# Experts' rows weighted on ScalarE and added by the scatter into two DRAM tables

## The reference

```python
topk_w, topk_i = jax.lax.top_k(tmp_scores, K)               # T x 6
flat = topk_i.reshape(-1)
pos = jnp.sum(jnp.cumsum(oh, axis=0) * oh, axis=-1) - 1     # oh: one-hot of flat
slot = flat * C + jnp.minimum(pos, C - 1)                   # C = 96
buf = jnp.zeros((E * C, H), x.dtype).at[slot].set(x[tok]).reshape(E, C, H)
g = jnp.einsum('ech,emh->ecm', buf, Wg)
u = jnp.einsum('ech,emh->ecm', buf, Wu)
out = jnp.einsum('ecm,ehm->ech', jax.nn.silu(g) * u, Wd).reshape(E * C, H)
yk = out[slot].reshape(T, K, H)
y = jnp.sum(yk * topk_w[..., None], axis=1)
return y + shared          # shared: one dense expert that all tokens pass
```

## Time and profile before

| | before |
|---|---|
| median of 3 runs, us | 1561.48 (1559.58 to 1565.09) |
| span of the profiled execution, us | 1556.1 |
| PE busy, us | 1394.1 (90%) |
| DVE busy, us | 1047.9 (67%) |
| ACT busy, us | 814.5 (52%) |
| POOL busy, us | 374.1 (24%) |
| DMA moved | 215.08 MB, mean 138 GB/s |
| of it on POOL's queue (q0) | 36.90 MB, 8.0% of 16 engines' span |

### The profile page before, as it was taken

The page is one execution under the profiler, slowest core; times in us unless marked ns, Lnnn a source line. Parts: engine busy times, 40 slices in busy tenths (PEclk is TensorE's granted clock), DMA queues, the critical chain, the costliest instruction groups (busy, mean ns, idle before and its releaser), DMA issues. The chain is left out here.

```text
span 1556.1 us, 36410 instructions
## 1 busy us (share of the span) xinstructions
PE 1394.1 (90%) x12869; PEld 982.9 (63%) x12869; DVE 1047.9 (67%) x2191; ACT 814.5 (52%) x1682; POOL 374.1 (24%) x796
## 2 busy tenths in 40 slices
PE   3848999999679999999989999999998798799977
PEld 2414555554556777777777677777767745599963
DVE  4856777764778888888822888888882378422228
ACT  1316665655327877777711877787770116222330
POOL 0434665530021111111110101111101000577730
PEclk9969999999889999999999999999999799799985
DMA  3038999872025655565620665566651430599948
GB/s 101 1 68 170 248 246 248 214 160 52 1 79 113 143 138 138 133 142 133 138 59 1 129 141 134 135 142 138 138 128 31 133 95 1 162 290 288 289 135 295
DMA packets 463401, 215.08 MB, mean 138 GB/s; under 512 B 412082, under 2 KB 434448, under 8 KB 463072
## 3 DMA queue, kind: packets, MB, share of 16 engines
q1 hardware_dynamic: 448992, 175.09, 47.0%
q0 software_dynamic: 12000, 36.90, 8.0%
q10 hardware_dynamic: 2336, 2.16, 0.4%
HBM read 81.97 MB, written 31.52 MB: 73 GB/s over the span
## 5 line engine op out<-in xcount | busy, mean ns | idle before, releaser
L1073 PE MATMUL bank<-a_pt,v_part 128*128 128x128 f16 x3456 | 235.3, 220 | 13.9 <-DMA a_pt<-a_ph 8.9
L1136 ACT ACTIVATE a_ph<-a_p,a_rinv 128x1024 f16<-128x1024 f32 (+7 forms) x256 | 198.7, 777 | 79.3 <-POOL a_rinv L1015 75.7
L755 DVE TENSOR_REDUCE a_qh<-bank 128x1 f16<-128x1024 f32 (+7 forms) x256 | 182.3, 755 | 85.0 <-PE bank L645 83.3
L1073 PEld LDWEIGHTS bank<-a_pt,v_part 128*128 128x128 f16 x3456 | 208.9, 98 | 47.2 <-DVE z_part L1163 7.5
L1144 DVE TENSOR_REDUCE a_negm<-bank 128x1 f32<-128x1024 f32 (+7 forms) x256 | 191.7, 749 | 55.9 <-PE bank L1057 55.7
L1052 PE MATMUL bank<-a_k,a_q 128*128 128x512 f16 (+3 forms) x1152 | 228.7, 326 | 0.2
L743 ACT ACTIVATE a_p<-bank 128x1024 f32<-128x1024 f32 (+7 forms) x256 | 157.8, 649 | 128.7 <-PE bank L700 113.3
L1178 DVE SCALAR_TENSOR_TENSOR a_ph<-a_p,a_rinv,a_ph 128x1024 f16<-128x1024 f32 (+7 forms) x256 | 206.8, 808 | 1.7 <-ACT a_ph L1136 1.7
L1125 ACT ACTIVATE a_p<-bank,a_negm 128x1024 f32<-128x1024 f32 (+7 forms) x256 | 189.3, 739 | 21.6 <-DVE a_negm L1144 21.6
L1015 POOL TENSOR_TENSOR a_rinv<-a_rinv,p_scale 128x1 f32<-128x1 f32 x256 | 48.8, 191 | 610.6 <-DVE a_rinv L1157 610.4
L924 PE MATMUL bank<-x_part,wsplit 128*128 128x512 f16 x768 | 186.0, 379 | 4.1 <-PEq L199 1.8
(11 more groups left out here) (206 smaller groups left out, 2230.9 us busy)
## 6 DMA issues: line engine op xcount, KB each, us to landing
wgu<-in_wgu SPq DMA_DIRECT2D x64, 352.0 KB
choice_rows<-zero POOLq DMA_DIRECT2D x24, 512.0 KB, 4.9
c_rows<-choice_rows SPq DMA_DIRECT2D x16, 768.0 KB, 11.2
wsplit<-w_parts POOLq DMA_DIRECT2D x30, 384.0 KB, 3.8
wd<-in_wd SPq DMA_DIRECT2D x64, 176.0 KB
pw_in<-in_wqkv SPq DMA_DIRECT2D x16, 384.0 KB, 4.9
w_parts<-pw_part SPq DMA_DIRECT2D x16, 384.0 KB, 2.9
a_pt<-a_ph SPq DMA_TRANSPOSE x256, 3.0
```

Source lines behind the costliest of these rows:

```text
L755: dve.tensor_reduce(qh[s][:, i, MC:MC + 1], s1_place(t), AX.X, ALU.max, negate=True).then_inc(m_ready, 1)
L1073: ins = eng.matmul(Z_ps[:, cols], g.vs[par][v_][:, k, :], turned[slot][:, a * blocks[j] + k, :], start=(k == 0 and (v_, a) == PARTS[0]), s ...
L1136: eng.activation(parts[slot][:, 0:w_], probs[slot][:, 0:w_], ACT.Copy, scale=rinv[:, p_, jj:jj + 1]).then_inc(p_hi, 1)
```

## The change

`choice_rows` goes. In its place stand two DRAM tables `token_sums0` and `token_sums1`, with one row per token and 128 spare rows. The scatter of expert e adds its rows into table e % 2 (`compute_op=ALU.add`), and before it is issued GpSimd waits until the previous scatter into that table, that of expert e - 2, has landed. Empty slots and the last slot now go to the spare rows.

So that rows can be added, they must be weighted first. `token_rows` gets 64 more columns and is doubled: its first half holds each token's `masked_scores`, the second half, which the last slot gathers from, holds ones. ScalarE's evacuation takes the expert's column of the gathered row as its scale. The normalized rows are therefore written twice, in eight transfers, and two further SyncE transfers write the 64 columns in the router.

The gather for expert e + 16 no longer waits for TensorE's transposes. The zeros are 10 writes in place of 24 (eight of 512 KB and two of 128 KB). In the tail SyncE loads two tiles of one table at a time, 16 transfers of 256 KB; GpSimd adds the two tables' parts, VectorE adds the late tokens' share from TensorE (eight tiles of it ahead) and then GpSimd's sum. The diagonal matrices and the multiply-adds go.

```diff
-        g.zero = sb("zero", [P, K * T * D // P // ZD])
-        g.xrows = nc.dram_tensor("token_rows", (T, D), F32, kind="Internal").ap()
-        g.krows = nc.dram_tensor("choice_rows", (K * T, D), F32, kind="Internal").ap()
+        g.zero = sb("zero", [P, 4 * D])
+        g.xrows = nc.dram_tensor("token_rows", (2 * T, D + E), F32, kind="Internal").ap()
+        g.sums = [nc.dram_tensor(f"token_sums{a}", (T + P, D), F32, kind="Internal").ap() for a in range(2)]
...
                 if kind == "keep":
-                    xv = g.xrows.rearrange("(n p) d -> p n d", p=P)
+                    xv = g.xrows.rearrange("(a n p) d -> a p n d", p=P, a=2)[:, :, :, 0:D]
                     for q in range(4):
                         sp.wait_ge(s_xn, N0 + 4 * q + 4)
-                        sp.dma_start(xv[:, 4 * q:4 * q + 4, :], xn[:, 4 * q:4 * q + 4, :]).then_inc(s_kept, 16)
-                    sp.wait_ge(s_kept, 64)
+                        for a in range(2):
+                            sp.dma_start(xv[a, :, 4 * q:4 * q + 4, :], xn[:, 4 * q:4 * q + 4, :]).then_inc(s_kept, 16)
+                    sp.wait_ge(s_kept, 128)
...
-                zv = g.krows.rearrange("(z p n) d -> z p (n d)", p=P, z=ZD)
+                def clear(z):
+                    rows = g.sums[z % 2][z // 2 * 4 * P:min(z // 2 * 4 * P + 4 * P, T + P), :]
+                    n = rows.shape[0] // P
+                    pool.dma_start(rows.rearrange("(p n) d -> p (n d)", p=P),
+                                   g.zero[:, 0:n * D]).then_inc(g.s_zero, 16)
...
-                        pool.dma_start(zv[m - 4], g.zero[:, :]).then_inc(g.s_zero, 16)
+                        clear(m - 4)
...
+            sp.wait_ge(s_msc, 1)
+            wv = g.xrows.rearrange("(a n p) d -> a p n d", p=P, a=2)[:, :, :, D:D + E]
+            sp.dma_start(wv[0], msc[:, :, :]).then_inc(s_kept, 16)
+            sp.dma_start(wv[1], ones[:, :].unsqueeze(1).to_broadcast([P, NT, E])).then_inc(s_kept, 16)
...
+            dve.nop().then_inc(s_msc, 1)
...
             dve.wait_ge(s_used, K)
-            dve.tensor_copy(g.src[:, :], picked[:, 0, :])
-            chained(dve.tensor_copy(dtmp[:, 0, :], picked[:, 0, :]))
-            chained(dve.scalar_tensor_tensor(dtmp[:, 0, :], picked[:, 1, :], float(T), dtmp[:, 0, :],
-                                             ALU.mult, ALU.add))
-            chained(dve.tensor_scalar(dtmp[:, 1, :], picked[:, 1, :], 0.5, float(OOB), ALU.is_lt, ALU.mult))
-            chained(dve.scalar_tensor_tensor(dtmp[:, 0, :], dtmp[:, 1, :], last[0:C, 0:1], dtmp[:, 0, :],
-                                             ALU.add, ALU.add))
+            dve.tensor_scalar(g.src[:, :], picked[:, 0, :], last[0:C, 3:4], None, ALU.add)
+            dve.tensor_scalar(dtmp[:, 0, :], picked[:, 0, :], last[0:C, 0:1], last[0:C, 2:3], ALU.mult, ALU.add)
+            chained(dve.tensor_scalar(dtmp[:, 1, :], picked[:, 1, :], 0.5, last[0:C, 1:2], ALU.is_lt, ALU.mult))
+            chained(dve.tensor_tensor(dtmp[:, 0, :], dtmp[:, 0, :], dtmp[:, 1, :], ALU.add))
...
+            pool.wait_ge(s_kept, 32)
...
-    rows = [g.sb(f"x_rows{i}", [C, XG, D], F32, c) for i in range(XB // XG)]
+    rows = [g.sb(f"x_rows{i}", [C, XG, D + E], F32, c) for i in range(XB // XG)]
...
             for i in range(NR):
-                sp.wait_ge(s_scat[i], ROWS_IN * (E // XB))
                 sp.wait_ge(s_out[i], 16 * (E // XB) + 16)
             c_load(sp)
...
-                                        bounds_check=T - 1, oob_is_err=False).then_inc(s_row[e % XB // XG], 16)
+                                        bounds_check=2 * T - 1, oob_is_err=False).then_inc(s_row[e % XB // XG], 16)
             for e in range(XB):
                 gather(e)
             for e in range(E):
                 pool.wait_ge(s_o, e + 3)
-                pool.indirect_dma_start(out=g.krows, out_offset=bass.IndirectOffsetOnAxis(
+                if e >= 2:
+                    pool.wait_ge(s_sum[e % 2], 16 * (e // 2))
+                pool.indirect_dma_start(out=g.sums[e % 2], out_offset=bass.IndirectOffsetOnAxis(
                     ap=g.dst[:, e:e + 1], axis=0), in_=orow[e % XB // XG][:, e % XG, :], in_offset=None,
-                    bounds_check=K * T - 1, oob_is_err=False).then_inc(s_scat[e % XB // XG], 16)
+                    compute_op=ALU.add).then_inc(s_sum[e % 2], 16)
                 if e >= XG and e % XG == 2:
-                    done = e // XG - 1
-                    pool.wait_ge(s_scat[done % NR], ROWS_IN * (done // NR + 1))
+                    for a in range(2):
+                        pool.wait_ge(s_sum[a], 16 * (XG // 2) * (e // XG))
                     pool.nop().then_inc(s_free, 1)
                 if e + XB < E:
-                    pool.wait_ge(s_t, e // 2 + 1)
                     gather(e + XB)
-            for i in range(NR):
-                pool.wait_ge(s_scat[i], ROWS_IN * (E // XB))
+            for a in range(2):
+                pool.wait_ge(s_sum[a], 16 * E // 2)
+            c_pair(pool)
...
-                act.activation(orow[s // XG][:, s % XG, :], g.bank[2][0:C, s % 2, 0:D], ACT.Copy).then_inc(s_o, 1)
+                act.activation(orow[s // XG][:, s % XG, :], g.bank[2][0:C, s % 2, 0:D], ACT.Copy,
+                               scale=rows[s // XG][:, s % XG, ds(e + D, 1)]).then_inc(s_o, 1)
...
 def combine(g, c, out):
-    NB = 8
-    rows = [g.sb(f"c_rows{i}", [P, K, D], F32, c) for i in range(NB)]
+    NQ = NT // 2
+    part = [[g.sb(f"c_sums{a}_{q}", [P, 2, D], F32, c) for q in range(NQ)] for a in range(2)]
     last = g.sb("c_last", [E, D], F32, c)
-    s_g = [g.sem(f"c_load{i}") for i in range(NB)]
-    s_acc, s_st, s_l, s_mm, s_dg, s_xs = [g.sem(f"c_{n}") for n in ("acc", "store", "last", "mm", "diag", "sum")]
+    s_in = [g.sem(f"c_load{q}") for q in range(NQ)]
+    s_st, s_l, s_mm, s_ov, s_pair, s_x = [g.sem(f"c_{n}") for n in ("store", "last", "mm", "overflow", "pair", "sum")]
+    g.s_sum = [g.sem(f"x_sum{a}") for a in range(2)]
     ov = out.rearrange("b (n p) d -> p (b n) d", p=P)
-    kv = g.krows.rearrange("(k n p) d -> p n k d", n=NT, p=P)
+    sv = [g.sums[a][0:T, :].rearrange("(n p) d -> p n d", p=P) for a in range(2)]
+    def overflow_bank(t):
+        return g.bank[t % 8 // 2][:, t % 2, 0:D]
     def load(sp):
         sp.dma_start(last[:, :], g.lrows).then_inc(s_l, 16)
-        for t in range(NT):
-            if t >= NB:
-                sp.wait_ge(s_xs, t - NB + 1)
-            sp.dma_start(rows[t % NB][:, :, :], kv[:, t, :, :]).then_inc(s_g[t % NB], 16)
+        def fetch(a, q):
+            sp.dma_start(part[a][q][:, :, :], sv[a][:, 2 * q:2 * q + 2, :]).then_inc(s_in[q], 16)
+        sp.wait_ge(g.s_sum[0], 16 * E // 2)
+        fetch(0, 0)
+        sp.wait_ge(g.s_sum[1], 16 * E // 2)
+        fetch(1, 0)
+        for q in range(1, NQ):
+            for a in range(2):
+                fetch(a, q)
     def matmul(pe):
         pe.wait_ge(s_l, 16)
         for t in range(NT):
-            if t >= 4:
-                pe.wait_ge(s_xs, t - 3)
-            ps = g.bank[t % 4][:, 0, 0:D]
-            pe.matmul(ps, g.wovT[:, t * P:(t + 1) * P], last[:, :], start=True, stop=False)
-            pe.wait_ge(s_g[t % NB], 16 * (t // NB + 1))
-            pe.wait_ge(s_dg, t + 1)
-            for k in range(KD, K):
-                ins = pe.matmul(ps, g.diag[:, t, k - KD, :], rows[t % NB][:, k, :], start=False, stop=(k == K - 1))
-            ins.then_inc(s_mm, 1)
-    def weigh(dve):
-        for tiles in ((0,), *((t, t + 1) for t in range(1, NT - 1, 2)), (NT - 1,)):
-            for t in tiles:
-                dve.wait_ge(s_g[t % NB], 16 * (t // NB + 1))
-            for k in range(KD):
-                for j, t in enumerate(tiles):
-                    if k:
-                        dve.wait_ge(s_acc, KD * tiles[0] + len(tiles) * (k - 1) + j + 1)
-                    dve.scalar_tensor_tensor(g.x[:, t, :], rows[t % NB][:, k, :], g.wk[:, t, k:k + 1],
-                                             g.x[:, t, :], ALU.mult, ALU.add).then_inc(s_acc, 1)
-            for j, t in enumerate(tiles):
-                dve.wait_ge(s_acc, KD * tiles[0] + len(tiles) * (KD - 1) + j + 1)
-                dve.wait_ge(s_mm, t + 1)
-                dve.tensor_tensor(g.x[:, t, :], g.bank[t % 4][:, 0, 0:D], g.x[:, t, :], ALU.add).then_inc(s_xs, 1)
+            if t >= 8:
+                pe.wait_ge(s_ov, t - 7)
+            pe.matmul(overflow_bank(t), g.wovT[:, t * P:(t + 1) * P], last[:, :],
+                      start=True, stop=True).then_inc(s_mm, 1)
+    def pair(pool):
+        for q in range(NQ):
+            pool.wait_ge(s_in[q], 32)
+            pool.tensor_tensor(part[0][q][:, :, :], part[0][q][:, :, :], part[1][q][:, :, :],
+                               ALU.add).then_inc(s_pair, 1)
+    def add(dve):
+        def overflow(t):
+            dve.wait_ge(s_mm, t + 1)
+            dve.tensor_tensor(g.x[:, t, :], overflow_bank(t), g.x[:, t, :], ALU.add).then_inc(s_ov, 1)
```

(59 more changed lines are left out.)

## The result

The changed kernel takes 1596.8 us (median of 4, 1590.3 to 1598.4) against 1562.6 us for the kernel before, measured on the same chip: a ratio of 1.0218, 95% interval 1.0190 to 1.0245. It is slower, by 34 us; 1570.5 had been forecast, and the time lies near the far rival's 1601. The profiled execution has a span of 1596.7, 40.6 more than before. That is more than the 34, because an execution's time is 1.7 above its span, and the profiled execution of before (1556.1) was 4.8 faster than the median of before, that of after 1.6 slower than its own.

The account below looks back on a forecast made before the run. Engine chain in the router, TensorE with DMA close behind in the expert loop, DMA loads in the tail; -26.5 + 6.1 + 0 + 0 + 1.0 + 28.4 = +9.0 us, forecast 1570.5, range 1545 to 1603.

Parts of the forecast that it names:

- far rival: Slow adding: queue occupied twice a plain row's time, landing 8 to 9 us under load, 1601 us; chance 0.19.
- By waits +28.4: Expert loop: scatters wait on GpSimd for the landing two before, holding up gathers, then TensorE; +28.4 us including the last 16.
- I take 0.4, near nothing: Loop: what adding was taken to lengthen a scatter's landing under load, 0.4 us, making 6.2.
- stretch (c): Loop, last 12 scatters with a gather, all weights asked for: GpSimd's own 2.53, say 2.6 each, 31.2 us.
- (a): Loop, first some 15 scatters, while the gathers' lead is used up: spacing 3.49, 52.4 us.
- (b): Loop, next 20 scatters, TensorE waiting for rows and weights asked for at GpSimd's pace: spacing 3.2, 64 us.
- Last 16: Last 16 scatters, no gather and idle queues: (0.78 + 2.35 + 0.3)/2 = 1.72 each, 27.4 us, a change of -0.4.
- The rule weighed there: Skill's fit for GpSimd-issued DMA: 2.2 us estimated per scatter, so waits cost nothing and the loop term is 0.
- Norm store +6.1: Norm before the router: token rows written twice, another 2.1 MB at 345 GB/s with nothing to cover it, +6.1 us.
- Zeros and weight columns 0: Zeros in first attention were hidden, nothing comes back; router's weight columns have 68 us of cover: 0 each.
- Tail: Behind the last scatter's landing: 4.2 MB loaded in place of 12.6, 24.4 us in place of 50.9, -26.5.
- Router 0: Router: weight columns queue behind expert weights on SyncE, covered for 68 us until the first gather; change 0.

Follow-up runs that it names:

- waits alone: The changed kernel with its scatters writing plainly in place of adding, the waits on the scatter two before kept: 1576.0 us, ratio 1.0101.
- adding alone: The kernel before, its scatters adding to zeroed rows of their own, with no wait on another scatter: 1588.3 us, ratio 1.0178.
- norm's wait moved: The changed kernel with the wait for both token-row copies moved from the norm's end to GpSimd at the router's end: 1592.0 us, ratio 1.0185.
- four tables: The changed kernel with four tables, each scatter waiting for the one four before, the end adding only two tables: 1567.5 us, ratio 1.0035.
- without waits and adding: The changed kernel with four tables, waits on the scatter four before, and plain writes in place of adding: 1543.7 us, ratio 0.9871.
- float16 rows: The kernel before with float16 choice rows, four of six weighted by TensorE, the norm's wait at the router's end: 1536.0 us, ratio 0.9818.

## Why the prediction was right or wrong, point by point

- **Sign and range right, size short by 26 us.** The mechanism forecast (a wait on GpSimd that the gathers, then TensorE queue behind) is there: TensorE first waits for rows at 1418.54, at about expert 24 (28 forecast). It is half of the loss. By waits +28.4 was forecast for the loop and the last 16, and waits alone cost 25.3 in the loop; with them alone the kernel takes 1576.0, so the sign is no luck, but the forecast holds only half of the cost.
- **The step that failed is the price of adding.** "I take 0.4, near nothing" was put into the landing only. Idle, the landing went from 2.35 to 3.36, so +1.0; half of that is the scatter's own time on GpSimd, 0.94 to 1.44, which costs every step whether anybody waits or not. I bounded the adding as a matter of the queue and kept GpSimd's 2.53 for stretch (c). In truth its step became 3.03 in every stretch, and 47 x 0.5 = 23.5 is what adding alone cost (23.9). The far rival's 1601 came near by chance: it wanted landings of 8 to 9 us from the queue, and they were 7.1 to 7.6.
- **The landing under load was short too, by the plain write's part.** 5.8 was taken for it, between a store's 5.4 and a gather's 7.77. The chain of plain writes has 6.5 to 6.8, about halfway between these rows. With adding the changed kernel's chain has 7.1 to 7.6 from 1378 to 1411; from 1377 to 1415 the median is 6.8 with the norm's wait moved and 7.2 with four tables, against 6.5 with plain writes. That is 0.3 to 0.7 for adding, so 0.4 was no bad value inside the landing. By the stretches of the prediction the changed kernel took 58.0 for (a), 70.9 for (b) and 37.1 for (c), where 52.4, 64 and 31.2 were forecast; with plain writes it was 47.5, 64.9 and 31.7. In (a) plain writes were faster than forecast although each landed later, because its first scatters landed sooner (3.6 us at 1365.5, 5.5 to 5.7 at 1373 to 1380).
- **Last 16.** The formula held, its landing didn't: (0.78 + 3.36)/2 = 2.07 gives the 2.09 measured, where 1.72 was forecast; four tables or plain writes give 28.7 and 28.2.
- **The rule weighed there fails under load.** Plain idle landings of 2.35 agree with the fit of about 2.0 us and bytes at 436 GB/s (the Trainium skill, "DMA: Bandwidth & Descriptors", section "Anatomy of one DMA — SWDGE (gpsimd) path"); the 6.5 to 6.8 of plain writes beside weight loads don't.
- **Norm store +6.1: exact, and by the mechanism forecast.** From 1230 to 1240 the DMA engines move 341 GB/s at a share of 1.02, where 345 was taken. It shows as SyncE's wait for `token_rows`, grown from 3.3 to 4.8, behind a longer issue. **Zeros and weight columns 0**: without waits and adding the kernel takes 1543.7, so at most some 2 us are left for them to cost. **Start of the loop +0.5** of 1.0 forecast.
- **Tail -25.3, -26.5 forecast: near, but by two errors that cancel in part.** The last load landed at about 1588.2, 17.1 us behind the landing of the last scatter, where the prediction's terms make 20.1 (2.9 + 17.0 + 0.2; the line there prints the second alone). The last sum, adds and store took 4.0 to 1592.2, 4.3 forecast. The 4.5 from there to the end of the span had no term: GpSimd's DRAIN holds the end of the block until 1596.45. Without it the tail would have given some 29 (an estimate from these times). The later landing of the last scatter, +1.0, stands in a row of its own.
- **Two slips in the prediction's numbers.** The 5.4 between span and median does not lie around the span: that is 1.7, and the rest is that the profiled execution was a fast one. The forecast, a difference put on the median, isn't touched. And 7.77 for all 47 gives +82, not +85.
- **Router 0: wrong by 3.7 in this trace.** The router's own work is the same; the granted clock isn't (below).

## What to carry to other kernels

When a DMA gets a new job, price it twice: once as the time until it lands, and once as the issuing engine's own time. Where that engine already runs at about the pace of the bound one, as GpSimd does here, half a microsecond per instruction is as dear as all the waits. A wait on a landing is to be priced at the load under which it lands, from transfers in the same stretch. If it must be waited for, more buffers in turn (here four tables in place of two) hide it, but what the further buffers cost elsewhere has to be in the sum. Where work goes to another engine at the end of a block, look at what that engine still does behind its last instruction. Before letting a queue add, see whether half the bytes buy the same at the end: here float16 rows did, without touching the loop.

## What the runs showed of the hardware that was not expected

- An indirect scatter of 96 rows occupies GpSimd for 0.94 us when it writes and 1.44 when it adds, in every kernel here, loaded or idle, with rows of 1 KB or 512 bytes (1431 ns on the mean in the changed kernel with float16 tables, 939 in the kernel before with float16 rows).
- At the end of the experts' block GpSimd's DRAIN lasts 8.2 to 8.5 us in the variants of the changed kernel that add and 11.9 to 12.1 in those that write plainly (7.0 and 10.5 in the kernel before, with adding and without). It starts when GpSimd's last work has been issued. In the kernel before that is 40 us ahead of the end and costs nothing; in the changed kernel it ends 4.2 us behind the landing of the last store, and with plain writes on two tables 7.0. What it waits for the traces don't show.
- The same router code ran in one of two lengths in the variants of the changed kernel: 103.6 us (the changed kernel, four tables that add, norm's wait moved) or 100.2 (the others). In 1272 to 1282 the granted clock was 0.66 in the changed kernel, between its two levels of 1.2 and 2.4 GHz, and 1.00, the upper level, in the one with plain writes. The window of the first (us, TensorE's busy time and count, PEclk, DMA share, GB/s), then that of the second:

```profile
1272.00:1282.00 10.00, 6.96 (x10) 0.66 0.41 106
```

```profile
1272.00:1282.00 10.00, 8.71 (x21) 1.00 0.41 106
```

Both lie about 30 us behind the router's start. Taken exactly from 30 to 40 us behind it, the clock is 0.66 in the three long ones and 1.00 in the four short ones, and TensorE is busy 6.8 to 7.0 us in all seven. What decides between the two was not found; it is 3.4 of the 40.6 us. Each length is that of one execution, and it may not belong to the kernel: of the changed kernel's four executions three had a mean granted clock of 0.937 to 0.939 and took 1595 to 1598 us, and one had 0.946 and took 1590.3.
